# Second attention: the attends go behind the maxima and the keys' stack, directly ahead of the local scores

## The reference, cut to what matters

```
v = x @ w_v + b_v
wq, wk = split(x @ w_wqk + b_wqk);  q, k = split(x @ w_qk + b_qk)
wdots = wq wk^T * 8**-0.5 + w_bias          # within windows of 64 tokens ("local")
dots  = q k^T + g_bias                      # over all 256 tokens ("global")
out = (softmax(wdots) v + softmax(dots) v) @ w_out + b_out
```

## Time and profile before

| | |
|---|---|
| time, median of 3 runs | 1450.89 us (1449.8 to 1456.36) |
| profiled execution, span | 1467.2 us (the page gives no other time of this execution) |
| busy share: PE, DVE, ACT, POOL | 89%, 77%, 66%, 51% |
| second attention, first keys' stack to last attend | about 774 to 1246 us of the span |
| one batch in the middle of it (global scores of r = 1 to the same of the next batch) | 960.05 to 988.90 us |

### The profile page before, as it was taken

How to read it: one execution, slowest core, us unless ns; L and a number is a source line. 1 busy time by engine, 2 the same in 40 slices (tenths; PEclk the granted TensorE clock), 3 DMA queues, 4 the chain that set the end, 5 groups by cost and what they waited for, 6 DMA issues and landing times. The chain is left out here.

```text
span 1467.2 us, 34194 instructions
## 1 busy us (share of the span) xinstructions
PE 1305.1 (89%) x12121; PEld 987.2 (67%) x12121; DVE 1130.4 (77%) x3054; ACT 969.6 (66%) x1498; POOL 751.3 (51%) x961
## 2 busy tenths in 40 slices
PE   2899999999998689899927999999999998699997
PEld 1566666666654367899915777777777776588886
DVE  5578889889875667899956888888888776567776
ACT  1688888888886447777723777777777777343441
POOL 4775665787852363799866455455444220101112
PEclk9899999999998779999958999999999999799999
DMA  6000000111111021122121111111111110134353
GB/s 234 18 23 20 22 20 20 28 32 28 31 36 30 8 80 32 56 73 73 58 87 51 49 47 48 46 48 47 49 46 38 39 42 18 26 92 116 80 129 82
DMA packets 84430, 77.20 MB, mean 53 GB/s; under 512 B 18224, under 2 KB 72240, under 8 KB 83888
## 3 DMA queue, kind: packets, MB, share of 16 engines
q1 hardware_dynamic: 80176, 66.73, 17.1%
q0 software_dynamic: 4096, 8.40, 2.0%
HBM read 36.26 MB, written 13.63 MB: 34 GB/s over the span
## 5 line engine op out<-in xcount | busy, mean ns | idle before, releaser
L541 ACT ACTIVATE a_p<-a_ps_s 128x1024 f32<-128x1024 f32 x256 | 258.3, 1031 | 25.1 <-PE a_ps_s L400 22.2
L651 DVE TENSOR_REDUCE a_qt<-a_ps_d 128x2 fp32r<-128x512 f32 x256 | 174.6, 687 | 48.9 <-PE a_ps_d L411 44.9
L1298 DVE TENSOR_REDUCE a_qt<-a_ps_d 128x2 fp32r<-128x512 f32 x256 | 173.3, 688 | 44.9 <-PE a_ps_d L1086 39.9
L822 POOL TENSOR_TENSOR a_rn<-a_ss,a_half 128x16 f32<-128x16 f32 x56 | 162.6, 2920 | 1.3
L1203 ACT ACTIVATE a_pg<-a_ps_s 128x1024 f32<-128x1024 f32 x128 | 125.8, 1024 | 26.8 <-PE a_ps_s L1075 25.4
L418 PE MATMUL a_ps_o<-a_p,a_v 128*32 128x256 f32 x2048 | 129.5, 393 | 3.7 <-ACT a_p L541 3.7
L1086 PE MATMUL a_ps_d<-a_kpad,a_qs 128*128 128x512 f32 x256 | 126.0, 495 | 5.8 <-DVE a_qt L1298 2.7
L411 PE MATMUL a_ps_d<-a_kpad,a_qs 128*128 128x512 f32 x256 | 126.8, 496 | 4.3 <-DVE a_qt L651 2.4
L2300 ACT ACTIVATE f_s<-f_ps_g 128x512 f32<-128x512 f32 x72 | 43.0, 598 | 99.9 <-PE f_ps_g L2246 99.7
L1494 POOL DMA_INDIRECT a_picked<-ys,rows x64 | 67.6, 1056 | 61.8 <-PE a_ps_d L1086 50.8
L418 PEld LDWEIGHTS a_ps_o<-a_p,a_v 128*32 128x32 f32 x2048 | 61.2, 112 | 52.9 <-issue 22.3
(11 more groups left out here) (355 smaller groups left out, 3823.9 us busy)
## 6 DMA issues: line engine op xcount, KB each, us to landing
a_kpad<-a_kc SPq DMA_DIRECT2D x512, 32.0 KB
f_gb<-spread SPq DMA_DIRECT2D x64, 256.0 KB, 5.7
a_kpad<-a_kq SPq DMA_DIRECT2D x256, 32.0 KB, 1.8
f_xin<-xs SPq DMA_DIRECT2D x39, 128.0 KB, 2.1
ys<-f_yout SPq DMA_DIRECT2D x39, 128.0 KB, 2.1
w<-in_w SPq DMA_DIRECT2D x2, 2304.0 KB, 11.4
out_x<-X SPq DMA_DIRECT2D x8, 256.0 KB, 6.8
xs<-f_zero SPq DMA_DIRECT2D x15, 128.0 KB
```

Of the source, the lines that this page charges most:

```text
L541: nc.scalar.activation(probs[:, u % 2, 2 * c:2 * c + 2, :, :].rearrange("p a b c -> p (a b c)"), ps_s[:, 2 * c:2 * c + 2, :].rearrange("p ...
L651: nc.vector.tensor_reduce(qt2[:, (k - PEAK) % 4, 2 * part:2 * part + 2, SHIFT], bank(k, f"m{part}")[:, :].rearrange("p (a b) -> p a b", b= ...
L822: nc.gpsimd.tensor_tensor(rn[:, part * c:(part + 1) * c], ss[:, part * c:(part + 1) * c], half[:, 0:c], ALU.pow).then_inc(rn_ready, 1)
L1298: nc.vector.tensor_reduce(qt[:, b % 2, GLOBAL, n:n + 2, SHIFT], bank(k, f"m{part}")[:, :].rearrange("p (j s) -> p j s", s=S), AX.X, ALU.ma ...
```

## The change

In TensorE's list, the second maximum, the keys' stack and the third maximum (with all that they wait for) move from behind the attends to ahead of them. The attends then stand between the third maximum and the local scores. In ScalarE's list, the keys' copy `kc` and the attends' copy `ot` change places accordingly. VectorE, GpSimd and SyncE keep their lists, and no instruction is added or removed.

```
                 maxima(k, 0)
+                maxima(k, 1)
+                if a_live(k, "K"):
+                    if k + KEYS == 0:
+                        pe.wait_ge(consts, 1)
+                    pe.wait_ge(stacks_ready, 2 * ((k + KEYS) // NG + 1))
+                    wait_a(k, "K")
+                    stack(kt, k + KEYS)
+                maxima(k, 2)
                 if unit(k - ATTENDED):
                     u = k - ATTENDED
...
                     last.then_inc(o_full, 1)
-                maxima(k, 1)
-                if a_live(k, "K"):
...
-                    stack(kt, k + KEYS)
-                maxima(k, 2)
                 if unit(k - SCORED):
                     pe.wait_ge(exp_done, exps_of(k, 2))
                     scores(k, WINDOWED, P)
...
                     global_exp(k, 1)
-                if unit(k - ATTENDED):
-                    act.wait_ge(o_full, attends(k))
-                    nc.scalar.copy(ot[:, :], ps_o[:, :]).then_inc(o_copied, 1)
                 if a_live(k, "K"):
                     act.wait_ge(a_full, a_count(k, "K"))
                     nc.scalar.copy(kc[:, (k + KEYS) % K_RING, :, :].rearrange("p a s -> p (a s)"), ps_a[:, :]
                                    ).then_inc(a_done, 1)
+                if unit(k - ATTENDED):
+                    act.wait_ge(o_full, attends(k))
+                    nc.scalar.copy(ot[:, :], ps_o[:, :]).then_inc(o_copied, 1)
```

## The result

The changed kernel takes 1484.99 us (median of 4 runs, 1481.06 to 1486.22), the kernel before 1450.93 beside it: a ratio of 1.0216, 95% interval 1.0187 to 1.0245. 1476 was forecast, with a range of 1456 to 1492.

What follows compares the result with a forecast made beforehand. TensorE was taken to bound the kernel; losses in batches 1 to 12 (22.9 us), the last three (1.9) and batch 0 (0.2) made +25.0 on 1450.9, so 1476 us, with an 8-in-10 range of 1456 to 1492.

Steps and rivals of the forecast that it cites:

- TensorE sets the pace: Second attention: TensorE, busy 39.7 of 40 us and strictly in order, loses time at each new wait; +25.0 us in all.
- r = 0: Steps with k % 4 = 0: m1 waits for projection `k`'s read-out, m2 for m0's reduction; +1.03 us.
- Pitches: Start-to-start times on TensorE without waits: m0 to m3 falls from 3.34 to 3.14, a gain of 0.20 us a step.
- r = 3: Steps with k % 4 = 3: m2 waits for m0's reduction, the least cost of any step; +0.16 us.
- r = 1: Steps with k % 4 = 1: the keys' stack waits for ScalarE's copy of `xT`; +0.52 us.
- r = 2: Steps with k % 4 = 2: m1 waits for `wq`'s read-out, +0.62 us, reduced to +0.20 at the O transposes.
- The count: Sum over the stage: 12 batches at 1.91 us, late batches 1.9, batch 0 0.2; +25.0 us.
- GpSimd's keys: GpSimd's queue in the second attention: its gathers wait for m0 alone, so no new wait; costed at nothing.
- ScalarE's swap: ScalarE's exchanged `kc` and `ot` copies: one fills waiting time, the other is covered by TensorE's work; costed at nothing.
- The first rival: Second attention: attends were badly placed, no new waits; 12.2 us gained plus O's waits of 3.4, 1435 us; chance 0.07.
- The backlog of r = 0: Rival on VectorE: earlier reductions dissolve its backlog, leaving 0.16 us in each of 61 steps, 1461 us; chance 0.15.
- The dear pitch: Rival: attends to local scores takes 0.80 us (+15), and nothing comes back at O; 1496 us; chance 0.12.

Runs made afterwards that it cites:

- before's second profile: The unchanged kernel profiled once more, to check its stage start and step lengths: 1454.24 us.
- r = 2 alone: The kernel before with the new order only in steps with k % 4 = 2: that step +0.97 us.

## Why the forecast was right, point by point

*TensorE sets the pace, and its list stops where a bank is late.* Shown: stages, step lengths and waits agree, the new order in one step alone lengthens that step, and taking r = 0's waits away gave 0.89 us of that step back. The sizes were too small throughout: +25.0 us forecast, +30.2 in the stage, +34 in the medians.

*Pitches.* Attends to local scores took 0.55, as taken. m0 to m1 was misread: 0.73 less 0.50 takes the second matmul of a merged row to be as long as a single one, but it lasts 0.40. m1 starts 0.33 after m0 and the stack 0.24 after m1, where the working had 0.23 and 0.34. That the sum of the two, 0.57, is right is luck, and only this sum counts in the forecast. One pitch was missed: m2 to the attends is 0.43 where m2 has waited for m0's reduction (r = 0 and 3), for the 0.40 taken, so the gain there was 0.17 and not 0.20, which makes most of r = 3's +0.18 for +0.16.

*r = 0: +1.07 for +1.03.* Both waits at the foretold places, and of the foretold length.

*r = 1: +0.63 for +0.52.* The right wait, mis-sized. TensorE at r = 1, then ScalarE's copy:

```profile
987.67 0.51 PE L1075 MATMUL a_ps_s<-a_qsm,a_kc 32*128 32x256 f32 x8
...
989.66 0.63 PE L1064 MATMUL a_ps_a<-ident,a_kt 128*128 128x128 f32 x4 [0.61 <-ACT a_xT L1213]
990.05 0.47 PE L1086 MATMUL a_ps_d<-a_kpad,a_qs 128*128 128x512 f32 x1
990.45 1.07 PE L1144 MATMUL a_ps_o<-a_pg,a_v 128*32 128x256 f32 x16
```

```profile
989.15 0.37 ACT L1213 COPY a_xT<-a_ps_a 128x256 f32<-128x256 f32 x1
```

The copy ends at 989.52 and the stack starts 0.14 later; I had carried over VectorE's 0.06. That is 0.08 of the 0.11. The other 0.03 is the stack to m2, 0.39 for 0.36; m2 to the attends is 0.40 here, as taken.

*r = 2: +0.40 for +0.20.* From m1 on it went as forecast: m1 to m3 2.91 us in both, and O without a wait. But m1 goes 1.84 us after the global scores (995.16 and 997.00):

```profile
995.16 0.51 PE L1075 MATMUL a_ps_s<-a_qsm,a_kc 32*128 32x256 f32 x8
...
997.00 0.50 PE L1086 MATMUL a_ps_d<-a_kpad,a_qs 128*128 128x512 f32 x1 [0.77 <-DVE a_proj L1321]
...
999.91 0.50 PE L1086 MATMUL a_ps_d<-a_kpad,a_qs 128*128 128x512 f32 x1
...
1001.20 0.66 PE L1165 MATMUL a_ps_d<-ident,a_ot 128*128 128x128 f32 x4
```

where 968.50 - 966.90 = 1.60 was foretold. VectorE reads `wq` later by 0.24, after two operations that run longer than in before:

```profile
994.32 0.80 DVE L1391 TENSOR_TENSOR a_mix<-a_picked,gates 128x512 f32<-128x512 f32 x1
...
995.85 0.75 DVE L1420 TENSOR_TENSOR a_out<-a_both 128x64 f32<-128x64 f32 x1
996.53 0.41 DVE L1321 SCALAR_TENSOR_TENSOR a_proj<-a_ps_d,a_bwq 128x256 f32<-128x256 f32 x1
```

In before's second profile:

```profile
950.80 0.68 DVE L1391 TENSOR_TENSOR a_mix<-a_picked,gates 128x512 f32<-128x512 f32 x1
...
952.22 0.63 DVE L1420 TENSOR_TENSOR a_out<-a_both 128x64 f32<-128x64 f32 x1
952.77 0.41 DVE L1321 SCALAR_TENSOR_TENSOR a_proj<-a_ps_d,a_bwq 128x256 f32<-128x256 f32 x1
```

0.12 each, which is the 0.24. GpSimd works beside both, in before as well, but with other pieces of its list. That its work can hold VectorE up, the other traces show: the multiplication (L1391 here) takes 0.68 again in all twelve cases of the kernel with the mixing early at r = 1, where no cast of GpSimd's runs beside it, and the sum of the attends' two results (L1420 here) takes 0.21 to 0.23 in every trace wherever GpSimd has nothing beside it. Which piece costs how much is open.

*The count.* 12 x 2.28 = 27.4 of the stage's 30.2; the rest, 2.8, are the late batches and batch 0, for which I had 2.1. The medians differ by 34 and the stages by 30; the stage's start and the work behind it vary by more than the 4 us between.

*A term put at nothing: GpSimd's keys.* "Neither queue gets a new wait" asks what GpSimd's queue waits for, and not when it delivers. The walk has the stack of r = 2 at 968.84, and one row of before has the keys out at 969.54 only. With r = 2 alone this made +0.97 for +0.20. That it came out harmless in the full change is luck: nothing in the working looked at it.

*ScalarE's swap, put at nothing.* It held: among TensorE's waits of after from 790 to 1230 us, all that ScalarE ends are those for `xT`, one of 0.8 us at L1055 and two of 0.5 together at the scores, and the last two stand in before's first profile too.

*The rivals.* The first rival's saving in pitches is real (0.17 to 0.20 a step), but the waits eat it: r = 3, with the cheapest wait, is already at +0.18. The backlog of r = 0 did not dissolve by itself; it went only when VectorE's list was changed. The dear pitch did not come.

## What to carry to other kernels

Work that stands between two users of a small ring of buffers is cover for the reader that empties it: before moving it, note for each task that moves ahead when its buffer, its operands and their makers on every engine are ready, and take the latest of these, also where no wait shows today. A wait that is just met is seen as a start within a tenth of a microsecond of a maker's end, and no view of waits lists it. A row that merges two instructions hides where the second starts; a narrower window shows it. One late task removed shows the next one, so the gain of an edit is not to be added to that of another without a run of both.

## What the runs showed that was not expected

- A release is not of one length: TensorE started 0.05 to 0.06 us after the end of a reduction or of a projection's read-out on VectorE, 0.06 after GpSimd's keys (990.63 to 990.69), and 0.14 after ScalarE's copy of `xT`. It doesn't go by engine: over all traces it is 0.15 where a maximum waits for VectorE's read-out of O (18 cases), and 0.05 in 3 cases where scores wait for ScalarE's global exponential. What sets it is open.
- The same VectorE operation of the mixing took 0.68 us in before and 0.80 in after. GpSimd's casts run beside it in both, in after for longer, and there one of them took 1.07 for 0.88.
- Where the code ahead of the stage was the same, the stage started at 781 to 795 us, from one execution to the next; that is half of what was to be measured.
